# LayerNorm's small arithmetic between statistics and shift: on GpSimd instead of VectorE

## What is computed

```python
def _layernorm(x, axis=-1, eps=1e-05):
    m = jnp.mean(x, axis=axis, keepdims=True)
    v = jnp.var(x, axis=axis, keepdims=True)
    return (x - m) / jnp.sqrt(v + eps)
...
    q, k = elu(q * scale) + 1.0, elu(k * scale) + 1.0      # 16 heads of 16
    k_cumsum, kv_cumsum = cumsum(k, axis=1), cumsum(k * v, axis=1)
    y = q * kv_cumsum / clip(sum over a head of q * k_cumsum, 1e-3)
...
    h = gelu(lowprec_linear(x, w_fc, b_fc))                # block_quant on x and w_fc
    return lowprec_linear(h, w_proj, b_proj)               # block_quant on h and w_proj
...
    x = _layernorm(x + attention(x))
    x = _layernorm(x + ffn(x))
```

## Time and profile before

| | before |
|---|---|
| median of 3 runs | 321.7 us (321.41 to 323.46) |
| the profiled execution | 321.13 us |
| its span, first to last instruction | 319.3 us |
| mean granted TensorE clock | 0.951 of full speed |
| TensorE matmuls busy | 263.4 us (82%) |
| VectorE busy | 255.4 us (80%) |
| ScalarE busy | 169.1 us (53%) |
| GpSimd busy | 159.8 us (50%) |
| chain of work that ended last | DVE 50%, PE 25%, issue 13%, ACT 4%, DMA 3%, POOL 3% |

### The profile page before, as it was taken

How to read it: one execution, slowest core, us unless ns; L and a number is a source line. 1 busy time by engine, 2 the same in 40 slices (tenths; PEclk the granted TensorE clock), 3 DMA queues, 4 the chain that set the end, 5 groups by cost and what they waited for, 6 DMA issues and landing times.

```text
span 319.3 us, 4631 instructions
## 1 busy us (share of the span) xinstructions
PE 263.4 (82%) x1476; PEld 164.8 (52%) x1476; DVE 255.4 (80%) x505; ACT 169.1 (53%) x278; POOL 159.8 (50%) x113
## 2 busy tenths in 40 slices
PE   5858964599899998999899989998999898768570
PEld 4515632276547554756466545664566445544350
DVE  2477745838989998899889988998899889867942
ACT  0633414235564856585657555764577547345242
POOL 0035242526364836573556555754666465575621
PEclk9799989759999999999999999999999999979987
DMA  6900002000200210010100120011001000100011
GB/s 178 348 1 3 0 1 66 0 2 1 66 0 2 68 51 17 0 63 9 60 0 21 45 66 0 0 66 66 0 0 66 0 0 2 66 0 3 0 67 66
DMA packets 13548, 11.70 MB, mean 37 GB/s; under 512 B 3040, under 2 KB 13280, under 8 KB 13536
## 3 DMA queue, kind: packets, MB, share of 16 engines
q1 hardware_dynamic: 11904, 11.28, 10.9%
q10 hardware_dynamic: 1632, 0.27, 0.5%
HBM read 7.35 MB, written 4.19 MB: 36 GB/s over the span
## 4 chain that ended last, share of the span: by engine, by line
DVE 50%; PE 25%; issue 13%; ACT 4%; DMA 3%; POOL 3%; SPq 0%; DVEq 0%; ACTq 0%; POOLq 0%
PE abank L900 11%; DVE h_amax L718 10%; DVE stats L692 7%; PE dbank L964 4%; DVE kf L653 3%; DMA h<-in_L_ffn_w_fc_dram 3%; DVE kvsum L670 3%; DVE h_pow L621 3%; DVE r L730 3%; DVE r L686 3%; DVE ksum L665 2%; PE bbank L932 2%; DVE hq L629 2%; DVE x_amax L708 2%; DVE kv L660 2%
## 5 line engine op out<-in xcount | busy, mean ns | idle before, releaser
L900 PE MATMUL abank<-xT,WqkvT 128*128 128x512 f32 x192 | 95.0, 622 | 25.3 <-DVE kf L653 21.0
L326 POOL TENSOR_TENSOR h_round<-h,h_inv 128x1024 f16<-128x1024 f32 x32 | 64.6, 2019 | 18.8 <-DVE h_inv L624 17.5
L900 PEld LDWEIGHTS abank<-xT,WqkvT 128*128 128x128 f32 x192 | 34.6, 196 | 60.9 <-DVE kf L653 28.0
L436 ACT ACTIVATE h<-hbank 128x512 f32<-128x512 f32 x64 | 37.5, 597 | 34.6 <-PE hbank L950 34.3
L311 POOL TENSOR_TENSOR rstd<-vareps,minus_half 128x4 f32<-128x4 f32 x16 | 17.4, 1090 | 55.4 <-DVE vareps L704 55.4
L302 POOL TENSOR_TENSOR qk<-qf,ksum 128x512 f32<-128x512 f32 x16 | 23.8, 1488 | 34.9 <-DVE ksum L665 29.2
L718 DVE TENSOR_REDUCE h_amax<-h 128x32 f32<-128x1024 f32 x32 | 38.6, 1208 | 1.7 <-ACT h L436 1.7
L950 PE MATMUL hbank<-w_fcT,xqT 128*128 128x512 bf16 x128 | 39.6, 392 | 0.0
L430 ACT ACTIVATE expz<-abank,zbias_neg 128x512 f32<-128x512 f32 x32 | 22.0, 688 | 33.1 <-PE abank L900 33.1
L446 ACT COPY hT<-tbank 128x512 uint32<-128x512 uint32 x32 | 18.6, 581 | 31.2 <-PE tbank L957 31.2
L964 PE MATMUL dbank<-w_prT,hT 128*128 128x256 bf16 x256 | 34.9, 282 | 0.0
(11 more groups left out here) (90 smaller groups left out, 425.5 us busy)
## 6 DMA issues: line engine op xcount, KB each, us to landing
x_sb<-in_L_attn_x_dram SPq DMA_DIRECT2D x8, 512.0 KB, 3.6
out_dram<-o_sb SPq DMA_DIRECT2D x7, 512.0 KB, 2.9
h<-in_L_ffn_w_fc_dram SPq DMA_DIRECT2D x1, 1024.0 KB, 10.1
h<-in_L_ffn_w_proj_dram SPq DMA_DIRECT2D x1, 1024.0 KB, 11.4
Wqkv_sb<-in_L_attn_Wqkv_dram SPq DMA_DIRECT2D x1, 512.0 KB, 6.5
out_dram<-o_sb SPq DMA_DIRECT2D x4, 128.0 KB, 1.7
Wqkv_sb<-in_L_attn_Wqkv_dram SPq DMA_DIRECT2D x1, 256.0 KB, 6.9
Wproj_sb<-in_L_attn_Wproj_dram ACTq DMA_DIRECT2D x1, 256.0 KB, 7.5
```

The source lines that it names most:

```text
L326: nc.gpsimd.tensor_tensor(h_round[:, t % 2].rearrange("p (g j) -> p g j", j=BLOCK_K), h[:, t].rearrange("p (g j) -> p g j", j=BLOCK_K), h_ ...
L436: nc.scalar.activation(h[:, t, half * HALF:(half + 1) * HALF], hbank[half][:, :], ACT.Gelu).then_inc(s_h, 1)
L900: last = nc.tensor.matmul(ps[:, :], WqkvT[:, k, e * P:(e + 1) * P], xT[:, k], start=(k == 0), stop=(k == CC - 1))
```

## The change

`mean_var` ends after the four `bn_stats`. `scale_shift` on GpSimd now waits for the statistics itself and does all that follows: three instructions from the statistics (difference and sum of the means, sum of the two sums of squares), three from these (the difference squared, the sum of squares times 4/C plus four epsilon, minus the sum of the means), their sum `var4`, which is four times the variance with epsilon, its power of minus one half, `half_rstd`, which is half of rstd, and from it rstd (added to itself) and shift. That is ten instructions on GpSimd in place of two, with waits on its own semaphores between the groups, and six fewer on VectorE, 16 times in the kernel. `s_sh` now counts two for each normalisation, so ScalarE's waits become 2n + 2. The order of all other work stays.

```diff
-            def scale_shift(S, vareps, rstd, negmean, shift, s_ve, s_rs, s_sh):
-
+            def scale_shift(S, stats, mv, var4, half_rstd, rstd, negsum, shift, s_st, s_mv, s_ve, s_rs, s_sh):
+
+                wait(pool, s_st, S + 1)
+                mean_e, m2_e, mean_o, m2_o = (stats[:, :, n] for n in (1, 2, 4, 5))
+                nc.gpsimd.tensor_tensor(mv[:, 1], mean_e, mean_o, ALU.subtract).then_inc(s_mv, 1)
+                nc.gpsimd.tensor_tensor(mv[:, 0], mean_e, mean_o, ALU.add).then_inc(s_mv, 1)
+                nc.gpsimd.tensor_tensor(mv[:, 2], m2_e, m2_o, ALU.add).then_inc(s_mv, 1)
+
+                wait(pool, s_mv, 6 * S + 3)
+                nc.gpsimd.tensor_tensor(mv[:, 3], mv[:, 1], mv[:, 1], ALU.mult).then_inc(s_mv, 1)
+                nc.gpsimd.tensor_scalar(mv[:, 4], mv[:, 2], 4.0 / C, 4.0 * LN_EPS, ALU.mult, ALU.add).then_inc(s_mv, 1)
+                nc.gpsimd.tensor_scalar(negsum[:, :], mv[:, 0], -1.0, None, ALU.mult).then_inc(s_mv, 1)
+                wait(pool, s_mv, 6 * S + 6)
+                nc.gpsimd.tensor_tensor(var4[:, :], mv[:, 4], mv[:, 3], ALU.add).then_inc(s_ve, 1)
                 wait(pool, s_ve, S + 1)
-                nc.gpsimd.tensor_tensor(rstd[:, :], vareps[:, :], minus_half[:, :], ALU.pow).then_inc(s_rs, 1)
+                nc.gpsimd.tensor_tensor(half_rstd[:, :], var4[:, :], minus_half[:, :], ALU.pow).then_inc(s_rs, 1)
                 wait(pool, s_rs, S + 1)
-                nc.gpsimd.tensor_tensor(shift[:, :], negmean[:, :], rstd[:, :], ALU.mult).then_inc(s_sh, 1)
+                nc.gpsimd.tensor_tensor(rstd[:, :], half_rstd[:, :], half_rstd[:, :], ALU.add).then_inc(s_sh, 1)
+                nc.gpsimd.tensor_tensor(shift[:, :], negsum[:, :], half_rstd[:, :], ALU.mult).then_inc(s_sh, 1)
...
             def norm_1(S, b):
-                wait(act, s_sh1, S + 1)
+                wait(act, s_sh1, 2 * S + 2)
...
-            def mean_var(S, r, stats, mv, negmean, vareps, s_r, n_r, s_st, s_mv, s_ve):
+            def mean_var(S, r, stats, s_r, n_r, s_st):
                 wait(dve, s_r, n_r)
                 for t in range(TILES):
                     last = nc.vector.bn_stats(stats[:, t], r[:, t])
                 last.then_inc(s_st, 1)
-
-                wait(dve, s_st, S + 1)
-                mean_e, m2_e, mean_o, m2_o = (stats[:, :, n] for n in (1, 2, 4, 5))
-                nc.vector.tensor_tensor(mv[:, 0], mean_e, mean_o, ALU.add)
-                nc.vector.tensor_tensor(mv[:, 1], mean_e, mean_o, ALU.subtract)
-                nc.vector.scalar_tensor_tensor(mv[:, 2], m2_e, C * LN_EPS, m2_o, ALU.add, ALU.add).then_inc(s_mv, 1)
-                wait(dve, s_mv, 2 * S + 1)
-                nc.vector.tensor_scalar(negmean[:, :], mv[:, 0], -0.5, None, ALU.mult)
-                nc.vector.scalar_tensor_tensor(mv[:, 3], mv[:, 1], 0.25, mv[:, 1], ALU.mult, ALU.mult).then_inc(s_mv, 1)
-                wait(dve, s_mv, 2 * S + 2)
-                nc.vector.scalar_tensor_tensor(vareps[:, :], mv[:, 2], 1.0 / C, mv[:, 3], ALU.mult, ALU.add).then_inc(s_ve, 1)
```

More of the change, by code:

```diff
@@ L129, in block_kernel @@
         stats1 = sb("stats1", [P, TILES, 6])
-        mv1 = sb("mv1", [P, 4, TILES])
-        negmean1 = sb("negmean1", [P, TILES])
-        vareps1 = sb("vareps1", [P, TILES])
+        mv1 = sb("mv1", [P, 5, TILES])
+        negsum1 = sb("negsum1", [P, TILES])
+        var4_1 = sb("var4_1", [P, TILES])
+        half_rstd1 = sb("half_rstd1", [P, TILES])
         rstd1 = sb("rstd1", [P, TILES])
@@ L157, in block_kernel @@
         stats2 = sb("stats2", [P, TILES, 6])
-        mv2 = sb("mv2", [P, 4, TILES])
-        negmean2 = sb("negmean2", [P, TILES])
-        vareps2 = sb("vareps2", [P, TILES])
+        mv2 = sb("mv2", [P, 5, TILES])
+        negsum2 = sb("negsum2", [P, TILES])
+        var4_2 = sb("var4_2", [P, TILES])
+        half_rstd2 = sb("half_rstd2", [P, TILES])
         rstd2 = sb("rstd2", [P, TILES])
@@ L213, in block_kernel @@
         s_mv1 = sem("mean_var1_ready")
-        s_ve1 = sem("vareps1_ready")
-        s_rs1 = sem("rstd1_ready")
-        s_sh1 = sem("shift1_ready")
+        s_ve1 = sem("var4_1_ready")
+        s_rs1 = sem("half_rstd1_ready")
+        s_sh1 = sem("scale_shift1_ready")
         s_x1 = sem("x1_ready")
@@ L232, in block_kernel @@
         s_mv2 = sem("mean_var2_ready")
-        s_ve2 = sem("vareps2_ready")
-        s_rs2 = sem("rstd2_ready")
-        s_sh2 = sem("shift2_ready")
+        s_ve2 = sem("var4_2_ready")
+        s_rs2 = sem("half_rstd2_ready")
+        s_sh2 = sem("scale_shift2_ready")
         s_o = sem("out_ready")
@@ L340, in scale_shift_1 @@
             def scale_shift_1(n):
-                scale_shift(n, vareps1, rstd1, negmean1, shift1, s_ve1, s_rs1, s_sh1)
+                scale_shift(n, stats1, mv1, var4_1, half_rstd1, rstd1, negsum1, shift1, s_st1, s_mv1, s_ve1, s_rs1, s_sh1)
             def scale_shift_2(n):
-                scale_shift(n, vareps2, rstd2, negmean2, shift2, s_ve2, s_rs2, s_sh2)
+                scale_shift(n, stats2, mv2, var4_2, half_rstd2, rstd2, negsum2, shift2, s_st2, s_mv2, s_ve2, s_rs2, s_sh2)
             round_w(0)
@@ L458, in norm_2_last @@
             def norm_2_last(n):
-                wait(act, s_sh2, n + 1)
+                wait(act, s_sh2, 2 * n + 2)
                 wait(act, s_ofree, n + 1)
@@ L466, in norm_1 @@
             def norm_1(S, b):
-                wait(act, s_sh1, S + 1)
+                wait(act, s_sh1, 2 * S + 2)
                 normalise(x1[:, b], r1, rstd1, shift1, s_x1)
             def norm_2(S):
-                wait(act, s_sh2, S + 1)
+                wait(act, s_sh2, 2 * S + 2)
                 wait(act, s_ofree, S + 1)
@@ L732, in mean_var_1 @@
             def mean_var_1(n):
-                mean_var(n, r1, stats1, mv1, negmean1, vareps1, s_r1, 2 * n + 2, s_st1, s_mv1, s_ve1)
+                mean_var(n, r1, stats1, s_r1, 2 * n + 2, s_st1)
             def mean_var_2(n):
-                mean_var(n, r2, stats2, mv2, negmean2, vareps2, s_r2, 4 * n + 4, s_st2, s_mv2, s_ve2)
+                mean_var(n, r2, stats2, s_r2, 4 * n + 4, s_st2)
             w_exponents(0)
```

## The result

| | before | changed |
|---|---|---|
| median | 321.73 us (321.41 to 323.46, 4 runs) | 337.38 us (336.46 to 339.0, 4 runs) |
| the profiled execution | 321.13 us | 336.46 us |
| its span | 319.3 us | 334.7 us |
| VectorE busy | 255.4 us (80%) | 251.0 us (75%) |
| GpSimd busy | 159.8 us (50%) | 186.4 us (56%) |

The ratio of changed to before is 1.047 (95% interval 1.042 to 1.052): 15.4 us more between the profiled spans, where 5.1 were forecast. The sign was as forecast; the size was three times as large and outside the range of 318 to 334. A ratio in this document is estimated from the single executions, without those more than 1.5% above the fastest of their kernel, and is not the quotient of the two medians.

What follows compares the result with a forecast made beforehand. VectorE (255.4 of 319.3 us busy) runs almost without a gap in the loop, otherwise waiting for TensorE or ScalarE's exponential. Six steps +1.7 and four outside norms +3.4 make +5.1: 321.7 to 326.8 us, range 318 to 334.

Steps and rivals of the forecast that it cites:

- GpSimd's free half would not carry it: Loop: GpSimd's idle time looks inviting, but rounding and num queued behind the norms delay VectorE; net +0.29 us a step.
- VectorE's gain of 0.61 at kf, 0.33 at den: Loop step: without six small instructions, kf starts 0.61 us earlier after the first norm, den 0.33 after the second.
- hq and the scans shut GpSimd out: Loop: VectorE's hq multiply and scans exclude GpSimd's reads; the second norm's last add is held until 203.36.
- a rounding shuts a scan out until 0.13 before its recorded end: First norm: the rounding of h keeps the scan of k out, making it 0.51 us late.
- the 0.22: Chance of nothing to measure: s about 0.10 (321.6 us), or a running rounding does not keep a scan out (323.8).
- s = 0.16: GpSimd: start-to-start distance in us of two small instructions that do not wait for each other; bounds 0.05 to 0.28.
- The chain without obstacle: GpSimd, last statistics to shift: 2.22 + 5s, so 3.02 us against 2.17 before, shift 0.85 later.
- A step: +0.29: Loop step: first norm gains 0.10 us, second loses 0.39; six steps give +1.7 us.
- The last step of the loop costs as much as the others: Loop: one step was walked and its +0.29 us taken for all six.
- Outside the loop, four times +0.85: First and last three norms: ScalarE waits for the shift, so each costs the whole +0.85 us, +3.4 together.
- The page's rule: GpSimd about twice as slow for two inputs: s = 0.23, total between the cases of s 0.20 and 0.28.
- the case of s = 0.28: Top of the rival of dear small instructions: 1.7 us a step, 10.2, plus 5.8 at the ends, 337.7; rival's chance 0.20.

Runs made afterwards that it cites:

- the kernel with the move: First norm of each loop step on GpSimd, rounding of h for tile 3 ahead of it, rest as before the change: 320.05 us, ratio 0.990.
- the run with tensor_tensor only: Changed kernel with its two tensor_scalar instructions replaced by tensor_tensor with a constant operand, epsilon left out: 330.21 us, ratio 1.020.
- the run with fillings: Changed kernel with 26 and 38 dummy transposes filling two TensorE idle gaps in the epilogue: 335.27 us, ratio 1.042.
- both moves together: Changed kernel with the rounding of h for tile 3 ahead of the first norm and second q times kv sum ahead of the second: 345.07 us.
- loop only: Changed kernel with the arithmetic on GpSimd only in the six loop steps, the other four norms on VectorE: 330.02 us, ratio 1.021.
- second norm only: Kernel before with only the second norm of each of the six loop steps moved to GpSimd: 329.65 us, ratio 1.025.

## Why the prediction was right or wrong

- **That GpSimd's free half would not carry it, and that the cost lies in what is queued behind the norm.** Right, and shown: by the rounding moved out of the way (first half of a step 0.60 us faster than before, where the order of the change gives +0.17), and by y's wait of 1.02 us for num.
- **VectorE's gain of 0.61 at kf, 0.33 at den.** Right. The first is 0.60 in the changed kernel's rows and the 0.60 of the kernel with the move; the second is 2.15 to 1.82, with den waiting 0.42 us for TensorE.
- **hq and the scans shut GpSimd out, and a rounding shuts a scan out until 0.13 before its recorded end.** Right, with 0.20 for the scan in place of the 0.13 taken from hq. The last was unproven, and its contrary had a share of the 0.22; the scan's 2.04 us settles it. The Trainium skill (SBUF — State Buffer, Who interferes with whom) calls the shared ports an exclusive lock, and says of VectorE's two-port modes that the first of the two keeps them for its whole instruction. The roundings bear that out for hq and the scan, which are no such mode, up to the last 0.13 to 0.20 us.
- **s = 0.16.** Right for tensor_tensor (0.155), wrong for two of the ten instructions. A tensor_scalar does not start before its predecessor has ended: 0.28. No row of before showed one on GpSimd in a group, and the prediction took all ten by the one kind that it had seen. That the strided reads cost nothing was right: the first group of three reads with strides, and its spacing is 0.155 as well. The chain without obstacle measured 3.27 us (327.13 to 330.40) where 3.02 was written: 0.24 from this, 0.03 from pow, recorded with 1.04 behind a tensor_scalar group and 1.01 without. In the loop it let the negation and not the last add meet hq and the scan, with the add still to come: 0.34 and 0.30 us of each step, by the run with tensor_tensor only. Why a tensor_scalar waits is not shown.
- **A step: +0.29.** Right as a mechanism, failed as a size: +0.82 on average over five steps. 0.64 of it comes from the two tensor_scalar, and with tensor_tensor only 0.18 was measured, so this term was mis-sized by its durations and not by its walk. That 0.18 lies below 0.29 is in part the scan, which got in 0.07 earlier than 0.13 before the rounding's end would have let it.
- **The last step of the loop costs as much as the others.** Failed: +2.68. In its second half den does not wait for TensorE (it starts 1.38 us after the statistics start, 1.82 in the steps before), so the scan of kv meets the chain earlier and more of the chain comes after it; y waits 1.57 us and is 0.82 later after the statistics than before, TensorE waits 3.13 and runs its next projections at the lower clock, which costs 1.67 by the run with fillings. With the 0.18 of the first half these make up the 2.68. The prediction had walked one step and multiplied it by six.
- **Outside the loop, four times +0.85.** Failed: +1.37, +1.51, +3.01, +1.16. Of the first nothing can be said: in the six other kernels whose norms there are those of before the stretch takes 37.34 to 38.48 us, against 37.01 before and 38.38 changed. The chain by itself is 1.10 later, about the +1.16 of the last; at N1(7) the last add is held up for another 0.48 by hq (shift done 3.76 us after the statistics, 2.23 before); at N2(6) the chain stands behind a rounding until 0.69 us after the statistics, its first instruction then waits for hq and so does pow (4.77 against 3.12). That is 1.65, and the other 1.36 of the 3.01 are TensorE at the lower clock from the transposes of hq on (6.81 us to N2(7), 5.45 at full clock). N1(7) to N2(6) also varies by itself: it is 24.25 with only the norms outside moved, 23.07 with all. The prediction had costed these four as a chain with no obstacle, with neither ports nor clock, although the same rule about hq that it used in the loop was at hand.
- **Start to N1(0), +1.57.** No step of the prediction, and not the change: the work there is the same. Over all the kernels profiled it was 47.31 to 50.92 us. It goes with the clock: the eight with a mean granted clock of 1.00 between 24 and 36 us reached N1(0) at 47.31 to 47.70, the four with 0.87 to 0.97 there, the changed kernel (0.95) among them, at 48.94 to 50.92. Which of the two brought the other about is not shown.
- **The page's rule, that GpSimd is about twice as slow for elementwise work.** The Trainium skill (GPSIMD Engine Reference, Engine selection) gave s = 0.23 and a total between 329 and 338. The 337.4 lies in that range, where the forecast's own did not hold it. But the rule was not shown to be right by its mechanism: the spacings within a group are 0.155 between tensor_tensor and 0.28 ahead of a tensor_scalar, none near 0.23, the dearer one stands ahead of the kind with one input where the rule is for two, and most of the miss came from outside the steady steps, which no s was asked for.
- **The range.** 318 to 334 left out the case of s = 0.28 (337.7) and gave a tenth to all beyond. That this case comes within 0.3 us of the measured 337.38 is luck: it had 10.2 us for six steps and 5.8 for the four norms outside, where 6.8 and 7.1 were measured, and 1.6 came ahead of any norm. Between the spans the forecast missed 10.3 us: 2.65 in the five steady steps, 2.39 in the last step, 3.65 in the four stretches around the norms outside (0.52, 0.66, 2.16, 0.31) and 1.57 ahead of N1(0). Three quarters lie where nothing had been walked, and for an error there the range had no room.

## What to carry to other kernels

Small arithmetic that moves to an idle engine brings its whole chain into that engine's queue: ask first what stands behind it there and who waits for that, then put whatever is already ready ahead of it. Here that one move turned +0.17 us in the first half of a step into −0.60. At the other norm, where the chain had to wait for what was put ahead, the second half took 2.2 to 2.7 us more than in the changed kernel; this was measured with both moves together. And walk the prologue, the last turn and the epilogue by themselves: a dependent chain has no cover there, and a wait of some 3 us (2.82 to 3.14, four kernels) was each time followed by TensorE's lower clock.

## What the runs showed of the hardware

- On GpSimd, 128x4 f32: tensor_tensor after tensor_tensor starts 0.155 us later, tensor_scalar 0.28 later, recorded with 0.19 to 0.23; a wait on the instruction before costs 0.08; pow took 1.01 to 1.04.
- A tensor_tensor_scan on VectorE with both operands in SBUF is kept out by a GpSimd rounding that already runs (2.04 us instead of 1.28, and 1.52 for the second scan of a step, which meets the rounding of x); it gets in 0.20 us before the rounding's recorded end.
- Ahead of the last output projections TensorE waited 2.82 to 3.14 us for y in four kernels (changed, loop only, second norm only, tensor_tensor only) and worked at its lower level soon after in all four. It waited 1.83 us in six and stayed at full clock in five of them; in the sixth, the first norm behind the rounding, it worked at its lower level (1.91 us for a group of four). With the gap filled it stayed at full clock.
- Steps of the loop repeat to 0.1 us from kernel to kernel (N1 to N2 is 16.95 to 17.00 us in every kernel that leaves it alone, over both steps of the body), while the start to N1(0) and N1(0) to N1(1) vary by 3.6 and 1.5 us without any change in them. A change worth under 1% of this kernel is read from the steps, not from the medians.
